# One elementwise pass of a weight quantisation moved from VectorE to GpSimd in a fused pre-norm transformer layer

## The reference

```python
def reference(x, Wq, bq, Wk, bk, Wv, bv, Wo, bo, w1, w2, w3):   # x: 1 x 2048 x 256, fp32
    h = layernorm(x)                                            # 16 heads of 16, causal, ALiBi bias
    q, k, v = heads(h @ Wq + bq), heads(h @ Wk + bk), heads(h @ Wv + bv)
    scores = q @ k.T / 4 + alibi_slope[head] * distance
    scores = where(causal, scores, lowest)
    x = x + merge(softmax(scores) @ v) @ Wo + bo
    def quantize(w):                                            # ternary weights: -1, 0, 1
        return clip(round(w / (mean(abs(w)) + 1e-8)), -1, 1)
    h = layernorm(x)
    hidden = sigmoid(h @ quantize(w1).T) * (h @ quantize(w2).T) # w1, w2: 704 x 256
    return x + hidden @ quantize(w3).T                          # w3: 256 x 704
```

## Time and profile before

| | |
|---|---|
| median of 3 runs | 629.21 us (628.88 to 631.59) |
| profiled execution | 630.86 us, its span 629.1 us |
| TensorE matmuls busy | 593.5 us, 94% |
| VectorE busy | 465.1 us, 74% |
| ScalarE busy | 364.4 us, 58% |
| Pool busy | 184.0 us, 29% |

### The profile page before, as it was taken

One profiled execution on the slowest core, in us unless ns is written; L12 is line 12 of the kernel. 1 busy time (PEld: TensorE's weight loads), 2 busy tenths in 40 slices (PEclk: granted clock), 3 DMA queues, 4 the chain that ended last, 5 costly groups with the idle time before them and its releaser, 6 DMA issues.

```text
span 629.1 us, 10829 instructions
## 1 busy us (share of the span) xinstructions
PE 593.5 (94%) x3452; PEld 365.8 (58%) x3452; DVE 465.1 (74%) x1206; ACT 364.4 (58%) x779; POOL 184.0 (29%) x394
## 2 busy tenths in 40 slices
PE   7888889999999999999999999999999999999987
PEld 5565456565657565655656565555555556556387
DVE  5978988677888776577897788788888888511177
ACT  3456457565554456666475465576676665676621
POOL 7646422362332241340212321203200400432500
PEclk9999999999999899999999999999999999999999
DMA  6885743651313116332141031173231210011001
GB/s 193 268 277 158 192 120 90 201 171 53 88 35 103 36 51 200 126 94 62 36 121 34 3 103 35 52 198 96 59 97 36 70 53 1 2 45 44 1 17 34
DMA packets 27452, 57.50 MB, mean 91 GB/s; under 512 B 5316, under 2 KB 14916, under 8 KB 23940
## 3 DMA queue, kind: packets, MB, share of 16 engines
q1 hardware_dynamic: 27396, 56.82, 31.6%
HBM read 40.69 MB, written 14.80 MB: 88 GB/s over the span
## 4 chain that ended last, share of the span: by engine, by line
PE 72%; DVE 16%; issue 5%; ACT 4%; POOL 1%; DMA 1%; ACTq 0%; POOLq 0%; DVEq 0%
PE pO L1132 19%; PE pS L1113 19%; PE pM L1092 16%; DVE pm L1302 5%; PE pM L1067 5%; DVE pM L1305 3%; PE pM L1000 3%; PE pM L1075 3%; ACT probs L915 2%; PE pM L1053 2%; PE pM L1008 2%; PE pS L1000 1%; PE pS L1067 1%; DVE work L1270 1%; DMA qst<-mT 1%
## 5 line engine op out<-in xcount | busy, mean ns | idle before, releaser
L915 ACT ACTIVATE probs<-pS 128x512 f32<-128x512 f32 (+3 forms) x640 | 300.7, 547 | 168.5 <-PE pS L1113 166.2
L1302 DVE TENSOR_REDUCE pm<-pM 128x1 f32<-128x512 f32 x384 | 239.2, 682 | 43.0 <-PE pM L1092 42.3
L1113 PE MATMUL pS<-qst,kst 128*128 128x512 f32 (+3 forms) x640 | 245.7, 403 | 7.2 <-ACT probs L915 4.6
L1092 PE MATMUL pM<-kst,qst 126*128 126x512 f32 (+3 forms) x640 | 228.8, 386 | 10.9 <-DVE pm L1305 4.4
L1113 PEld LDWEIGHTS pS<-qst,kst 128*128 128x128 f32 x640 | 119.0, 190 | 94.2 <-issue 47.5
L1092 PEld LDWEIGHTS pM<-kst,qst 126*128 126x128 f32 x640 | 120.0, 191 | 52.3 <-DVE pm L1302 14.9
L1305 DVE CUSTOM_DVE_ANT_0 pM<-pM,mask 128x128 f32<-128x128 f32 (+3 forms) x256 | 119.8, 524 | 36.5 <-PE pM L1092 36.2
L793 POOL TENSOR_SCALAR_AFFINE_SELECT probs<-probs 128x128 f32<-128x128 f32 x256 | 76.0, 309 | 221.5 <-ACT probs L915 213.9
L1132 PE MATMUL pO<-probs,vals 128*17 128x512 f32 (+3 forms) x1264 | 133.5, 540 | 0.0
L1132 PEld LDWEIGHTS pO<-probs,vals 128*17 128x17 f32 x1264 | 29.5, 97 | 65.0 <-issue 40.4
L1067 PE MATMUL pM<-x2T,wT 128*128 128x256 f32 x256 | 38.5, 292 | 1.5 <-DVE pm L1305 0.7
(11 more groups left out here) (154 smaller groups left out, 391.5 us busy)
## 6 DMA issues: line engine op xcount, KB each, us to landing
kst<-parts SPq DMA_DIRECT2D x78, 256.0 KB
qst<-parts SPq DMA_DIRECT2D x30, 256.0 KB, 3.9
parts<-qk_hl SPq DMA_DIRECT2D x28, 256.0 KB, 4.0
ctx_dram<-ctx_raw SPq DMA_DIRECT2D x15, 256.0 KB, 3.8
xin<-in_L_attn_x SPq DMA_DIRECT2D x5, 512.0 KB, 5.1
out<-work SPq DMA_DIRECT2D x8, 256.0 KB, 4.2
work<-ctx_dram SPq DMA_DIRECT2D x7, 256.0 KB
work<-rden_dram SPq DMA_DIRECT2D x7, 256.0 KB
```

Of the source, the lines that this page charges most:

```text
L915: nc.scalar.activation(probs[:, n % PSLOTS, q0:CH], pS[:, n % SBANKS, q0:CH], ACT.Exp)\
L1092: pe.matmul(max_bank(x)[:, 0:N], qst[0:R_MAX, u % QSLOTS, h, t * P:(t + 1) * P], kst[0:R_MAX, n % KSLOTS, h, 0:N], start=True, stop=True). ...
L1113: pe.matmul(pS[:, n % SBANKS, q0:CH], kst[0:R_END, sl, h, b:b + P], qst[0:R_END, u % QSLOTS, h, q0:CH], start=True, stop=True).then_inc(sc ...
L1302: nc.vector.tensor_reduce(dst, bank, AX.X, ALU.max).then_inc(max_free, 1)
```

## The change

The first passes of the ternary weights move from VectorE to Pool: after the clearings of steps 4, 6 and 8 Pool does both halves of one matrix and waits for them to finish. VectorE does the second passes at heads 1 and 3 of steps 5, 7 and 9, as before, and now waits for each half of the first pass by semaphore. The planner is told that steps 4, 6 and 8 are free of ternary work and that 5, 7 and 9 hold 1.9 us of it, in place of 1.5 us in each of the six. The memset of a part of `vals` gets a semaphore of its own.

```diff
+    TERN_AT, TERN_PIECES, GT_AT = [5, 7, 9], 2, [4, 6, 8]
...
-        if s in TERN_STEPS:
-            room -= 1.5
+        if s in TERN_AT:
+            room -= 1.9
...
+        def tern_piece(n, piece):
+            i = (2, 0, 1)[n]
+            t = (FT if i < 2 else KT) // TERN_PIECES
+            rows = slice(piece * t, (piece + 1) * t)
+            return i, tern_v[i][:, rows, :], w_rows[i][:, rows, :]
...
+            def first_comparisons(n):
+                if n == 0:
+                    need_empty(pool, ("gamma",))
+                if n == 1:
+                    pool.wait_ge(tern_ok, TERN_PIECES)
+                for piece in range(TERN_PIECES):
+                    i, dst, src = tern_piece(n, piece)
+                    nc.gpsimd.tensor_scalar(dst, src, thr[:, 0, i:i + 1], None, ALU.is_gt).then_inc(gt_ok, 1)
+                pool.wait_ge(gt_ok, TERN_PIECES * (n + 1))
...
+                if s in GT_AT:
+                    first_comparisons(GT_AT.index(s))
...
-            def ternary(n, half):
-                n, second = divmod(n, 2)
-                i = (2, 0, 1)[n]
-                t = (FT if i < 2 else KT) // 2
-                dst, src = tern_v[i][:, half * t:(half + 1) * t, :], w_rows[i][:, half * t:(half + 1) * t, :]
-                if not second:
-                    if n == 1:
-                        dve.wait_ge(tern_ok, 2)
-                    nc.vector.tensor_scalar(dst, src, thr[:, 0, i:i + 1], None, ALU.is_gt).then_inc(gt_ok, 1)
-                else:
-                    dve.wait_ge(gt_ok, 2 * n + 2)
-                    nc.vector.scalar_tensor_tensor(out=dst, in0=src, scalar=thr[:, 1, i:i + 1], in1=dst,
-                                                   op0=ALU.is_ge, op1=ALU.add).then_inc(tern_ok, 1)
+            def ternary(n, piece):
+                i, dst, src = tern_piece(n, piece)
+                dve.wait_ge(gt_ok, TERN_PIECES * n + piece + 1)
+                nc.vector.scalar_tensor_tensor(out=dst, in0=src, scalar=thr[:, 1, i:i + 1], in1=dst,
+                                               op0=ALU.is_ge, op1=ALU.add).then_inc(tern_ok, 1)
...
-                    if s in TERN_STEPS and h % 2:
-                        ternary(s - TERN_STEPS[0], h // 2)
+                    if s in TERN_AT and h % 2:
+                        ternary(TERN_AT.index(s), h // 2)
```

More of the change, by code:

```diff
@@ L374, in preln_layer @@
         gt_ok = sem("gt_ok")
+        vals_ok = sem("vals_ok")
         tern_ok = sem("tern_ok")
@@ L1413, in _ @@
                     dve.wait_ge(tern_ok, 6)
-                    nc.vector.memset(vals[:, T // P // 2:T // P, :, HD:VW], 1.0).then_inc(gt_ok, 1)
+                    nc.vector.memset(vals[:, T // P // 2:T // P, :, HD:VW], 1.0).then_inc(vals_ok, 1)
                 if ph == 5 and c >= 1:
```

## The result

The changed kernel is slower: 635.5 us median (634.2 to 636.4, 4 runs) against 629.05 us; the ratio is 1.0083, 95% interval 1.0056 to 1.011. The time lies outside the predicted range and on the other side of no change. The profiled execution has a span of 634.0 us against 629.1 us.

What follows compares the result with a forecast made beforehand. The prediction took TensorE, then from 56.6 us to step 9's end VectorE, as the bound. Step 2's gain and saved first passes, less waits for Pool, gave 1.4 us: 629.21 to 627.8 us, range 625.8 to 631.2 us.

Steps and rivals of the forecast that it cites:

- I take 0.8 us, since this has one input tensor: Price of each Pool compare half, from one-input casts and clearings; the other end, from two-input operations, was 1.9 us.
- first rival: Pool's halves cost the two-input price, 1.9 us; step 9's VectorE work ends at 78.0 us, total 633.8 us; chance 0.11.
- The port: VectorE's two-input second passes can't share SBUF access with Pool's compares, so both wait for both first passes; 0.8 us at stake.
- step 2's 0.95 us: With one turn fewer ahead, the values' projection in step 2 and step 4's scores start 0.95 us earlier.
- the DMA of w3 in time: Step 2: w3 arrives at about 46 us, so ScalarE's sum over it does not hold back the gain.
- VectorE as the chain of steps 6 to 9: From 56.6 us to the end of step 9 VectorE works without a gap and bounds the kernel before.
- the start of Pool behind the last exponential: Steps 4, 6, 8: Pool starts after the last clearing, which follows the last exponential; 53.9 us in step 4.
- a shift carried one for one to the end: Any shift at 73.4 us, the end of step 9's VectorE work, reaches the kernel's end in full.
- price of a first use: Pool's first compare was priced at no pause; a rival had 5 us and more, 633 us and up, chance 0.03.
- The sum for a price of 0.8 us: Steps 2 to 9 with 0.8 us halves: VectorE ends at 71.7 us against 73.42 us, gain 1.7 us.
- The whole saving: Rival: step 2's 0.95 us, 2.9 us of chain and no clock fall, 3.9 to 5.5 us, about 624.6 us; chance 0.11.
- The clock: TensorE's fall to 1.2 GHz from 76 to about 79 us, costing 1.7 us, stays; both signs are in the range.

Runs made afterwards that it cites:

- e3_cast: The changed kernel with Pool's compare replaced by a plain fp32 to bf16 cast; 628.40 us, ratio 0.9974 to the kernel before.
- e5_imm: The changed kernel with Pool's compare against a constant (0.4) instead of a scalar from memory; 633.24 us, a single run.
- e6_mult: The changed kernel with Pool's compare replaced by a multiplication by the same scalar; 635.10 us, a single run.
- e10_head3: The changed kernel with both second passes of a matrix at head 3 of steps 5, 7 and 9; 635.46 us, ratio 1.01 to the kernel before.
- e7_w2pool: The kernel before with the new distribution of turns and only w2's first pass on Pool, halves in steps 6 and 7; 625.54 us, ratio 0.9937.
- e4_early: The changed kernel with Pool's compares one step earlier, in steps 3, 5 and 7; 630.70 us, ratio 1.0016 to the kernel before.
- e8_unit2: The kernel before with the new distribution of turns for unit 2 alone (steps 2 to 5); 629.11 us, ratio 0.9996.
- e1_plan: The kernel before with the changed kernel's distribution of turns alone, both passes staying on VectorE; 627.18 us, ratio 0.9962.
- e9_nofirst: The changed kernel without any first pass, second passes adding to a buffer of ones; 625.68 us, ratio 0.9937 to the kernel before.
- e13_w2again: The same kernel as e7_w2pool, run once more for its time; 625.41 us, ratio 0.9944 to the kernel before.
- e12_w2old: The kernel before with only w2's first pass on Pool and the old distribution of turns; 627.18 us, ratio 0.9973.
- e2_oldplan: The changed kernel with the old distribution of turns; 636.23 us, ratio 1.0109 to the kernel before.

## Why the prediction was wrong

**The term that failed** is "I take 0.8 us, since this has one input tensor". It measured 2.04 and 2.20 us. The number of input tensors was the wrong key: the rows of casts and clearings gave 0.84 ns for an element, and e3_cast got just that, but e5_imm and e6_mult show that arithmetic with a scalar costs 2.5 ns for each further element on Pool, constant or not, compare or multiplication. With the right price in the same sums the forecast's own first rival comes out; it said 633.8 us for 1.9 us a half. Its chance of 0.11 was too low: the two bounds were a factor of 2.3 apart, and no row showed this instruction.

**The first rival's sum** ended at 78.0 us where 79.4 was measured. Pool's start in step 6 was 62.49 us (62.6 said), in step 8 73.86 us (72.2 said). The 1.7 us are in the main the fall of the clock at 68 us, which no step of the prediction had: in e5_imm, without that fall, Pool starts at 71.85 us. The halves of 2.20 in place of 1.9 us add 0.6 us, and the first second pass, which runs beside Pool's second half and not behind it, gives 0.9 us back. So the rival had the mechanism, and its sum was 1.4 us short at the end of step 9.

**The port** was half right. I had let both second passes start behind both first ones. They started behind the first half, at once, and ran 0.58 to 0.65 us longer beside the second half of 2.04 or 2.20 us (1.53 for 0.95, 1.65 for 1.00), which took no longer itself. By the Trainium skill (SBUF — State Buffer, section "SBUF: two separate sides") the second pass should have been blocked for the whole of Pool's instruction, until 58.16 us; it ended at 57.70. The measurement decides: beside this instruction VectorE is held for a part of it only. Which part, three other runs show, in which VectorE's pass starts later within Pool's compare:

```profile
56.50 1.18 DVE L1352 SCALAR_TENSOR_TENSOR work<-work,thr 128x704 bf16<-128x704 f32 x1
```

```profile
63.95 1.18 DVE L1351 SCALAR_TENSOR_TENSOR work<-vals,thr,work 128x768 bf16<-128x768 f32 x1
```

```profile
72.98 1.02 DVE L1352 SCALAR_TENSOR_TENSOR work<-work,thr 128x768 bf16<-128x768 f32 x1
```

In e10_head3 the pass starts 0.41 us behind the start of Pool's half and runs 0.23 us longer, in e7_w2pool 0.53 and 0.18 us, and in e4_early 0.69 us behind it and not longer at all. Start and lengthening add up to 0.64 us at 704 elements and 0.7 us at 768 each time: VectorE's pass gets going only 0.6 to 0.7 us behind the start of a compare of 2.04 or 2.20 us, and from there on runs as if alone. Beside e3_cast's cast of 0.77 us the same sum is 0.56 us (start 0.09 us behind, 1.42 us long). Beside the split of 1.28 us it is 1.05 us: started 0.14 us behind it w1's first pass takes 1.56 us (e8_unit2), 0.31 us behind it 1.40 us (before), 1.03 us behind it 0.66 us (e1_plan). The 1.40 us that the prediction put under the rule is of a pass with one input in SBUF, of which the rule as it is told there does not speak; only the 2.22 us, Pool's split with a two-input pass of VectorE in it, is a case of it.

**Right:** step 2's 0.95 us and its cause; the DMA of w3 in time (but for two profiled executions of other kernels); VectorE as the chain of steps 6 to 9 of the kernel before; the start of Pool behind the last exponential (54.08 us, 53.9 said); a shift carried one for one to the end (6.2 us at the marker, 6.5 us at the store of unit 6 and in the medians; in the other kernels marker and median differ by up to 1.6 us, and by 3.4 us in e7_w2pool, whose profiled execution had the wait for w3). Right too was that Pool has no price of a first use: the first compare, at 54.1 us, takes 2.04 us like the second. By the Trainium skill (GPSIMD Engine Reference, section "Instruction dispatch") the first call of freshly loaded code costs some 6 us more; no run here shows such a pause.

**The sum for a price of 0.8 us** said 1.4 us of gain; e3_cast gave 1.0 us by its median (628.40 against 629.39 us).

**The whole saving** was priced at 3.9 to 5.5 us; e9_nofirst, which has none of the first passes, gives 3.4 us. The 2.9 us of chain were 1.3 at the marker, after step 2's 0.95: behind VectorE, TensorE was next in line.

**The clock** was taken as a cost that stays. It was more: the change brought a second fall and a longer first one, and the kernels that gained most (e9_nofirst, e7_w2pool, e13_w2again) had none at 68 to 80 us in the profiled execution.

## What to carry to other kernels

Price an offloaded instruction by a row of the same instruction with the same kind of operands, and where there is none, carry both bounds through the sum; the choice between them decided the sign here. An engine with idle time on average has a place in its queue all the same: put a long instruction where its result is needed last and its data is there first, one piece at a time, as w2's two halves, and leave on the busy engine what is needed soon after its input is there. Before moving work, run the planner's part of a change by itself: here it was worth 0.4% and hid in a change that cost 0.8%.

## What the runs showed of the hardware

Pool's arithmetic with a scalar takes 2.04 us for 128x704 and 2.20 us for 128x768 fp32 to bf16, against 0.77 and 0.83 us for a cast of the same. A two-input pass of VectorE that starts together with it is lengthened by 0.6 us, not blocked for 2 us, and one that starts 0.69 us behind it is not lengthened.

TensorE's clock went to 1.2 GHz in or behind the pause ahead of step 10's transposes in eight profiled executions, with pauses of 1.21 to 4.60 us (before, the change, e1_plan, e3_cast, e4_early, e5_imm, e6_mult, e10_head3). It stayed at 2.4 GHz behind 0.54, 0.72, 0.98 and 1.00 us (e9_nofirst, e13_w2again, e12_w2old, e7_w2pool). In two kernels it fell before that pause began: in e2_oldplan at 77.8 us, behind one of 2.56 us that ended at 77.6, and in e8_unit2 at 71.6 us, behind one of 0.96 us that ended at 70.9. The sixteen weighted sums of step 10 took 1.70 us where the clock stayed and 2.3 to 3.2 us where it fell, so a fall there costs 0.6 to 1.5 us of matmul time.
